# Splitting 192 features as 128 + 64 in the first level's linear experts of a vision tower

## The reference

```python
h = h + _L0_ffn_ref(_layernorm(h), router_w, router_b, expert_w, expert_b)
```

## Time and profile before

| | |
|---|---|
| time, median of 3 runs | 1727.51 us (1727.13 to 1731.24) |
| profiled execution, its own time | 1732.31 us |
| its span | 1730.4 us |
| TensorE busy (matmuls) | 1401.0 us, 81% |
| VectorE, ScalarE, GpSimd busy | 644.4, 467.7, 464.5 us |
| granted TensorE clock, mean | 0.86 |

### The profile page before, as it was taken

The page is one execution under the profiler, slowest core; times in us unless marked ns, Lnnn a source line. Parts: engine busy times, 40 slices in busy tenths (PEclk is TensorE's granted clock), DMA queues, the critical chain, the costliest instruction groups (busy, mean ns, idle before and its releaser), DMA issues. The chain is left out here.

```text
span 1730.4 us, 35498 instructions
## 1 busy us (share of the span) xinstructions
PE 1401.0 (81%) x14426; PEld 1101.9 (64%) x14426; DVE 644.4 (37%) x1668; ACT 467.7 (27%) x1226; POOL 464.5 (27%) x597
## 2 busy tenths in 40 slices
PE   6468855999998799599998899668339995876998
PEld 6164433888875798488876589526329993453756
DVE  2445663433432122333342222355511124543424
ACT  0420242443442111243343111123103331422120
POOL 0010273322333243232232424224043441320000
PEclk9688865999998899799999899886559997857999
DMA  5010203100003432600000453240043552020000
GB/s 125 0 29 13 87 1 123 37 2 2 2 3 140 149 114 84 191 2 2 3 2 2 168 183 117 82 118 5 1 171 122 178 187 79 4 57 0 28 27 19
DMA packets 56096, 115.08 MB, mean 67 GB/s; under 512 B 16384, under 2 KB 43268, under 8 KB 50848
## 3 DMA queue, kind: packets, MB, share of 16 engines
q1 hardware_dynamic: 38848, 58.02, 11.3%
q0 software_dynamic: 17088, 54.81, 9.1%
HBM read 137.97 MB, written 24.87 MB: 94 GB/s over the span
## 5 line engine op out<-in xcount | busy, mean ns | idle before, releaser
L1296 PE MATMUL bank<-xT,w 96*128 96x512 f32 x192 | 86.2, 608 | 15.5 <-ACTq L1350 15.5
L1149 PE MATMUL bank<-t_ew,t_hg 128*128 128x192 f32 x552 | 97.2, 327 | 0.0
L1389 DVE SCALAR_TENSOR_TENSOR h<-bank,cw,h 128x192 f32<-128x192 f32 x128 | 53.5, 418 | 99.8 <-PE bank L1312 82.9
L1035 POOL DMA_INDIRECT t_ew<-in_t_moe,source x46 | 48.0, 1043 | 154.8 <-DVE t_og L1217 124.9
L1149 PEld LDWEIGHTS bank<-t_ew,t_hg 128*128 128x128 f32 x552 | 88.7, 190 | 0.2
L329 PE MATMUL bank<-ident,rows 128*96 128x128 f32 x112 | 25.4, 419 | 76.9 <-DVE rows L312 76.9
L1181 ACT ACTIVATE t_hg<-bank 128x384 f32<-128x384 f32 x92 | 40.1, 488 | 168.2 <-PE bank L1137 131.7
L1177 ACT ACTIVATE l_hg<-bank,l_ew 128x128 f32<-128x128 f32 x186 | 51.4, 375 | 122.6 <-PE bank L1137 82.4
L1296 PEld LDWEIGHTS bank<-xT,w 96*128 96x128 f32 x192 | 37.3, 196 | 60.3 <-issue 43.8
L1704 PE MATMUL bank<-t_wo,t_ctx 128*128 128x192 f32 x384 | 75.0, 348 | 0.5 <-ACT t_ctx L1798 0.4
L1133 PE MATMUL bank<-t_xgT,t_ew 128*128 128x128 f32 x552 | 70.8, 279 | 3.8 <-DVE t_xgT L1208 3.3
(11 more groups left out here) (329 smaller groups left out, 3028.3 us busy)
## 6 DMA issues: line engine op xcount, KB each, us to landing
rows_in<-blank SPq DMA_DIRECT2D x2, 2967.0 KB
t_xg<-rows_in SPq DMA_DIRECT2D x46, 129.0 KB
t_qkv<-in_t_wqkv SPq DMA_DIRECT2D x9, 576.0 KB
t_wo<-in_t_wo SPq DMA_DIRECT2D x8, 576.0 KB
w<-in_l_w SPq DMA_DIRECT2D x8, 576.0 KB, 5.4
rows_in<-blank SPq DMA_DIRECT2D x1, 3999.0 KB
l_xg<-rows_in SPq DMA_DIRECT2D x31, 129.0 KB
wA<-in_t_wqkv SPq DMA_DIRECT2D x2, 1728.0 KB
```

The lines of the kernel that those rows point to most:

```text
L1035: pool.indirect_dma_start(k.ew[i % W_SLOTS][:, 0:weights.shape[1]], None, weights, bass.IndirectOffsetOnAxis(ap=k.source[:, b:b + 1], axis=0),
L1149: mm = pe.matmul(k.bank[6 + b % 2][:, 0:DIM], k.hg[b % 2][:, m, :], w[:, SPLIT + m * DIM:SPLIT + (m + 1) * DIM], start=(m == 0), stop=(m = ...
L1296: mm = pe.matmul(k.bank[(u * FC + m) % 4][:], k.w1[s][:, c, m * P:(m + 1) * P], k.xT[:, c, n * HALF:(n + 1) * HALF], start=(c == 0), stop= ...
L1389: ins = dve.scalar_tensor_tensor(out, src, k.cw[:, tile, bass.ds(col, 1)], out, ALU.mult, ALU.add)
```

## The change

The first level's norm and router are called with `split=True`. The weights of the router and of the experts are laid out on the host for the new chunks (`split_rows`, `split_columns`). The expert phase takes the pairs of experts two at a time: first both pairs' matmuls on the first 128 features, each in its bank; then, for the last 64 features, one matmul on partitions 0 to 63 for the first pair and one on 64 to 127 for the second. Both banks are signalled behind these. VectorE's instructions and the barriers stay as they are.

```diff
             for t in range(NT):
+                toks = slice(t * P, (t + 1) * P)
                 for p in range(pairs + 1):
...
                     else:
-                        for c in range(2):
-                            mm = pe.matmul(k.bank[i % 8][:, 0:2 * DIM], k.xT[:, c, t * P:(t + 1) * P],
-                                           w[:, c, (p - 1) * 2 * DIM:p * 2 * DIM], start=(c == 0), stop=(c == 1))
-                    mm.then_inc(k.turned, 1)
+                        pe.matmul(k.bank[i % 8][:, 0:2 * DIM], k.xTs[:, 0, toks], w[:, (p - 1) * 2 * DIM:p * 2 * DIM],
+                                  start=True, stop=False)
+                        if p % 2 == 0:
+                            for o in range(2):
+                                half = slice(o * REST, (o + 1) * REST)
+                                col = (n_e + p - 2) * DIM
+                                mm = pe.matmul(k.bank[(i - 1 + o) % 8][:, 0:2 * DIM], k.xTs[half, 1, toks],
+                                               w[half, col:col + 2 * DIM], start=False, stop=True)
+                                mm.then_inc(k.turned, 1)
+                    if p == 0:
+                        mm.then_inc(k.turned, 1)
                     i += 1
...
-            we = tensor(st, "l0_we", [CH, 2, 8 * DIM])
+            we = tensor(st, "l0_we", [P, 12 * DIM])
...
-            norm_phase(k, k.h, 1e-5, loads=[(we[:], a["l0_we"]), (k.bout[0:8, :], a["l0_be"])])
-            router_phase(k, 8, 2, "probs", k.before[0], True, True)
+            norm_phase(k, k.h, 1e-5, split=True, loads=[(we[:], a["l0_we"]), (k.bout[0:8, :], a["l0_be"])])
+            router_phase(k, 8, 2, "probs", k.before[0], True, True, split=True)
...
-    a["l0_wr"] = k_major(i["L0_ffn_router_w"].T)
+    a["l0_wr"] = split_rows(i["L0_ffn_router_w"].T)
-    a["l0_we"] = k_major(i["L0_ffn_expert_w"].transpose(2, 0, 1).reshape(DIM, 8 * DIM))
+    a["l0_we"] = split_columns(i["L0_ffn_expert_w"].transpose(2, 0, 1).reshape(DIM, 8 * DIM), 2 * DIM)
```

More of the change, by code:

```diff
@@ L2107, in build @@
                       (k.cont[0][:], a["cont8"]), (k.cont[1][:], a["cont16"]),
-                      (k.wr[:, :, 0:8], a["l0_wr"]), (k.rb[:, 0:8], a["l0_rb"])]
+                      (k.wrs[:, :, 0:8], a["l0_wr"]), (k.rb[:, 0:8], a["l0_rb"])]
             embed_phase(k, patches, wtok, pos, tri01, consts,
```

## The result

The changed kernel takes 1726.65 us (median of 22 runs) against 1729.53 us for the kernel before (22 runs beside them, one of them at 2005.55 us, which hardly moves a median); the ratio is 0.998, with a 95% interval of 0.9972 to 0.9988, that is 3.5 us less (2.1 to 4.8). In a second comparison (12 runs, beside 17 of the kernel before, whose median was 1734.33 us there) the ratio was 0.9986 (0.9971 to 1.0002), or 2.4 us less; by itself this one doesn't tell the change from none. The forecast was 2.6 us less, or 1724.9 us from the 1727.51 us of the three runs known then; the measured median is 1.75 us above it, and that of the kernel before came out 2.0 us higher over 22 runs. The effect is clear of zero in the first comparison, and lies within the 0.3% that I called no change.

The account below looks back on a forecast made before the run. The three edited phases follow each other with barriers, TensorE limiting the expert phase; experts -4.5, router +2.3, norm +0.1, clock -0.5 give -2.6 us, from 1727.5 to 1724.9 us, range 1720.8 to 1729.0.

Parts of the forecast that it names:

- The array: Expert-phase matmuls: halves overlap, each arrangement change costs 0.2 us; a tile takes 5.19 us against 5.875.
- The last tile: End of expert phase: both banks come at once, VectorE needs 1.92 us and ends 0.33 us later than before.
- Rival 4: Expert phase: VectorE becomes the limit; at 1.25 us a bank a tile is 5.5 us, about 1727.3 us; chance 0.06.
- The router: First router: alternating 128 and 64 rows lengthens it from 5.55 to 7.4-8.3 us; +2.3 taken, bounds +1.8 and +3.1.
- rival 1: Router meets the low clock for all records (+3.1), expert-phase clock rises no sooner: 1726.2 us; chance 0.15.
- The clock in the expert phase: Clock rises 5.2 us after the expert phase's first matmul instead of 6.2, gaining 0.5 us.
- experts: Linear-expert phase: seven shorter tiles give -4.8 us, the later end of the last tile +0.3: -4.5 us.
- norm: First level's norm phase: eight added ScalarE copies and transposes both 128 wide cost +0.1 us.
- Rival 2: Expert phase: added boundaries hide under the preceding run, a tile takes 4.59 us, total 1720.1 us; chance 0.09.
- rival 3: Expert phase: halves do not run side by side, +1.29 us a tile, total 1735.2 us; chance 0.05.
- the phases after 191 us change length: Stated sign of a wrong prediction: phases after the edited ones change length, which nothing in the diff asks.

Follow-up runs that it names:

- experiment 1: Changed kernel with both half matmuls of a group on partitions 0 to 63, so one after the other: ratio 1.0071 to the kernel before.
- experiment 3: Changed kernel with all four pairs of a tile in one group, three changes of arrangement instead of five: ratio 0.9955 to the kernel before.
- experiment 7: Changed kernel with tiles from the third on run pair by pair, halves not side by side: 1741.26 us, one run.
- experiment 11: Four-pair version with both routers reordered, plus all eight bias matmuls moved ahead of the first tile: ratio 0.9948 to the kernel before.
- experiment 5: Changed kernel with one signal by two behind both halves instead of one behind each: 1732.55 us, one run.
- experiment 9: Changed kernel with the last 64 features padded by zero weights to 128 rows, no halves: 1732.59 us, one run.
- experiment 4: Changed kernel with four-pair groups (last tile two groups of two) and both split routers' 128-row matmuls first: ratio 0.9925 to the kernel before.
- experiment 8: Changed kernel and kernel before, both rerun unaltered: ratio 0.9986 for the changed kernel; the kernel before took 1731.86 us in one run.
- experiment 10: Changed kernel with the halves one after the other, run again for a second look at the clock: 1751.33 us, one run.
- experiment 6: Changed kernel with each pair's 128-row matmul followed at once by its own on partitions 0 to 63: ratio 1.0336 to the kernel before.
- experiment 2: Changed kernel with its first router's eight 128-row matmuls before its eight 64-row ones: ratio 0.9966 to the kernel before.

## Why the prediction was right

**The array.** Forecast 5.19 us a tile, measured 5.18. Its terms stand by themselves: overlap of the halves 1.28 us a tile (experiment 1), a change of arrangement 0.2 us at the upper clock (experiments 3, 7, 11: two fewer, four more, one fewer), and it is not the signals (experiment 5). With nothing but the layout changed there is no gain (experiment 9).
The Trainium skill's rule that a change of tiling mode drains TensorE ("TensorEngine Tiling (Array Packing)", Key Properties) agrees with this. A change costs 0.2 us here at the upper clock and 0.29 at the lower, between runs of 384 columns.

**The last tile.** Forecast: VectorE's last work 1.92 us after the banks are ready, and 7.18 us from the tile's bias matmul to the end. Measured 1.89 and 7.17.

**VectorE.** Rival 4 did not come: it waits 0.45 us at each group, and even at 4.27 us a tile it waits. The Trainium skill's warning on emptying PSUM ("TensorEngine Tiling (Array Packing)", PSUM Bottleneck) decides nothing at the changed kernel's pitch. In the last tile of experiments 4 and 11, where four banks are still being emptied, VectorE did set the time.

**The router.** Forecast 7.4 to 8.3 us with 7.85 taken; measured 7.38 in one profile and 8.41 in the other. The working had a slip: with 9 to 10 records before the clock falls it gives 7.4 to 7.7 us, that is +1.9 to +2.2 and not +2.3, and the first profile's 7.38 (+1.8) fits that. The size depends on whether the clock is up when it begins, which I had as a bound (+3.1, measured +2.9) and as rival 1; it is low in four of the nine profiles of the unordered split router (experiments 1, 7, 8, 10, against the first profile and experiments 3, 5, 9, where it took 7.38; experiment 6 had 7.18). I gave this too little weight.

**The clock in the expert phase.** Forecast 5.2 us to the rise, measured 4.3, 5.2 and 4.4 (experiment 5). Together with the array this makes the expert phase 45.5 to 45.9 us long, against 51.0 before: 5.1 to 5.5 less, forecast 5.0.

**The sum.** Forecast: experts -4.5, router +2.3, norm +0.1, clock -0.5, in all -2.6 us. Measured, with half a us for each us of the rise: -4.6, +1.8, +0.1 and -0.9 in the first profile, -3.6 in all; -4.6, +2.9, +0.1 and -0.5 in the second, -2.1 in all; the medians -3.5 (2.1 to 4.8) and -2.4. So the mechanism and its main term came as forecast. That the total lies between the two profiles is partly luck: which clock the router meets moves it by 1 us, and the rise by half a us. Rival 2 (no boundaries) and rival 3 (no overlap) are excluded by the tile pitch.

**What I did not foresee** is how much phases elsewhere move with an execution. I had written that the prediction is wrong if the phases after 191 us change length. In the first pair of profiles they did: from the next norm to the end the changed kernel took 3.7 us less. The sign was badly chosen, since experiment 8 shows the same kernel with both lengths. The stage from level 1's norm to its transformer block took 92.2 to 95.3 us, and the stage from the final norm of level 1 to level 2's attention 54.5 to 57.7, in code that is the same in all profiles. In both the length goes with the granted clock. The first took 92.2 us at a mean clock of 0.65 (experiments 4 and 7) and 95.0 to 95.3 at 0.61 to 0.62 (both kernels, both profiles); the second took 54.5 at 0.83 (experiment 4, the changed kernel's first profile) and 57.4 at 0.78 (its second, and experiment 7). That an edit moves the rise in these stages by moving their start is my reading; no run tested it. The spans of the profiles of experiments 4 and 8 differ by 12.0 us: 5.6 are the edited phases, 3.1 and 2.9 these two stages, and the others nearly cancel.

## What to carry to other kernels

Two matmuls on 64 rows side by side save one matmul's time, but every change between row arrangements cost 0.2 us in the expert phase and 0.10 to 0.13 us in the router: put as many matmuls of one arrangement in a row as the banks allow, in small side phases such as a router too. With four pairs to a group and both routers ordered the time was 0.75% below the kernel before instead of 0.2%; of that, the profiles show 7.7 us or 0.45% in the edited phases (the changed kernel's 2.1 and experiment 4's 5.6 more), and 1.5 of these 7.7 us hang on the clock that the first router met (5.55 us in experiment 4, 7.07 in experiment 2). Before moving narrow or half-row matmuls to the start of a phase, look at when the clock rises there: it can take back all that the pitch gains.

## What the hardware showed that I had not expected

The rise of the clock depends on the stream; that TensorE shows as busy is not enough. Time from the expert phase's first matmul until the granted clock left 1.2 GHz: 4.3 to 6.6 us with matmuls on 96 or 128 rows or with halves side by side; 22.4 and 22.2 us with every second run on one half of the rows; not at all in a phase of 109 us with the same halves one pair at a time; 10.1 us when 5.4 us of matmuls on 8 rows came first. Once at 2.4 GHz, the stream that could not raise it held it for the 43 us that were left (experiment 7). The late rise was seen twice (experiments 1 and 10), the others of these streams once each.
